# Layer norms of the next batch's x tiles: two at each of two head-group boundaries instead of four inside the first head group

## The chip, the cores and the metric

The kernel runs on one core of a Trainium2 chip. The metric is the time of one execution on the device, in microseconds (us); the median of several runs is compared. Engines are named as in the profile: PE (TensorE matmul), PEld (its weight load), DVE (VectorE), ACT (ScalarE), POOL (GpSimd), SP (SyncE, which issues all the DMAs).

## The reference

Input x is 8 batches of 512 rows by 512, and so is the context. The reference is two layers; the first step, the only one that the change touches, is a cross attention with 16 heads of 32:

```python
x = x + tanh(g_xattn[0]) * mha(layernorm(x), ctx, ctx, W_Q, b_Q, W_K, b_K, W_V, b_V, W_O, b_O)
x = x + tanh(g_ffn[0]) * bitlinear_ffn(layernorm(x), w_gate, w_up, w_down)
x = x + tanh(g_xattn[1]) * softmax(layernorm(x) @ ctx.T) @ ctx
x = x + tanh(g_ffn[1]) * (mxfp4(layernorm(x)) @ mxfp4(w1).T + bias)

def layernorm(x): m, v = mean(x), var(x); return (x - m) / sqrt(v + 1e-5)
def mha(Q, K, V, ...): q, k, v = Q @ W_Q + b_Q, K @ W_K + b_K, V @ W_V + b_V   # 16 heads of 32
    return softmax(q @ k.T / sqrt(32)) @ v                      # per head; the output projection follows
```

## The kernel before

The program has three stages one after another: `attention_phase` (about the first 880 us), `ffn_phase` and `final_phase`. Only the first is changed.

**The work of a batch.** An x tile is 128 rows of x (T = 4 of them, 256 KB each). It is loaded into one of four `stage` buffers (L288). Its layer norm is step "ln1" (DVE: `bn_stats` L514, `bn_aggr` L519; then four short POOL operations of one column, L580, L581, L584, L587) and step "norm" (ACT, L466, which writes the normed tile back into `stage`). PE transposes it (L344), ACT and DVE split the result into a high and a low part (`xt`, L449, L527). The four context tiles use the same four `stage` buffers after the x tiles, without a norm. Projections Q and K (L360) are made for each of four head groups (G = 4, four heads in each), with three passes each for precision; ACT (L458) and DVE (L535) read them out into `part`, which is written to DRAM (`spill`, L300) and read back, rearranged, into `stack` by three DMAs (`fill`, L308). V is projected in the first head group (L374).

**A head group** has 16 slots. In each PE computes one maximum product `mx` (L385; DVE reduces it to the row maximum, L543) for the next heads but a few, and one score product `sc` (L402; ACT takes the exponential into `probs`, L488). The 16 maxima are transposed (L391), copied by ACT (L479) and sent by a small DMA "mrow" (L314) into row 96 of `stack`, where the next group's scores need them. POOL sums `probs` over the four key tiles into `acc`: 12 additions of 128x512 per group (L597), the first when the fifth exponential is there. After the 16 slots come 16 products with V ("pv", L413) and then "den", the products of `acc` with ones (L423), which need the last POOL addition. DVE then takes reciprocals (L549, four of 128 columns), multiplies (L554), ACT adds the bias (L493), SP stores. "den" is in PE's order ahead of everything of the next group.

**The order of the work** is written out by hand. `Clock` holds steps with a time in units (PERIOD = 160 units for a head group, 640 for a batch; a slot is 8 units). Each engine takes the steps that are its own, adds its own lag (`late`), takes the times modulo 640 and issues them in that order, each behind its semaphore waits; a negative time is work for a later batch. So a step with time -636 is at position 4 of the window of the batch before, which is in head group 0; -827 is at position 453, after the last slot of head group 2. Nothing is issued before what is ahead of it on its engine. Batches 0 and 1 and the last two are written out; batches 1 to 5 of the window counter run in a hardware loop with four branches back.

Positions in a batch's window that matter here: the four groups begin at 0, 160, 320, 480; their pv and den at 128 to 156 behind that. DVE's first reciprocal of a group is 2 units into the next one. On SP the order in group 2 and 3 is: fill (392), store (406), spill (411), mrow (442), spill (448), fill (480), spill (516), load 0 (520), fill (520), load 1 (536), load 2 (552), fill (552), spill (553), store (566), load 3 (568), spill (590), fill (592), mrow for group 0 (602), spill (627), and two fills at 32 and 64 of the next window.

The waits that the text speaks of (all unchanged):

```python
wait_count(pe, acc_done, it, shift, G * (T - 1) * J, (g + 1) * (T - 1) * J)          # den
wait_count(act, ln_rstd, it, shift, T, i + 1)                                         # norm
stage_wait(dve, it, shift, i)                                                         # ln1
sync_wait(sp, held, t_full, it, shift, 2 * T, i - STAGE + 1)                          # load
wait_count(act, spilled[side], it, shift, G, g, 16)                                   # read-out of a projection
```

Of the kernel before, what the change touches and what calls it, by code (L numbers as in the profile page):

```python
# [125 lines left out]
def attention_phase(nc, NB, x, ctx_in, w_q, b_q, w_k, b_k, w_v, b_v, spill, attn_t):  # L126
# [11 lines left out]
    with ExitStack() as ctx:  # L138
        def sb(name, shape, dt):
            return ctx.enter_context(nc.sbuf_tensor("a_" + name, shape, dt))  # L140
# [8 lines left out]
        bias = sb("bias", [P, 3, G], F32)  # L149
# [57 lines left out]
        def ahead(n):  # L207

            return round(slot(int(n // 1)) + (n % 1) * U) - 3 * PERIOD

        at = dict(load=-760, load_step=16, ln1=-636, norm=-612, ln_step=24, tload=6, spill=20, act_norm=3, act_turn=4, dve_turn=8,
                  act_qk=6, dve_qk=11, act_v=8, dve_max=5, act_exp=5, mt=-46, mrow=8, act_mt=3, acc=12, pv=7, den=28,
                  recip=34, recip_step=16, norm_out=98, bias=108, store=118, pool_ln=7)
        tx_at, tc_at = (0, 1.5, 3, 4.5), (10.8, 12.3, 13.8, 15.3)
        qk_at = {(0, Q): 6, (0, K): 16.8, (1, Q): 21.4, (1, K): 26, (2, Q): 30.6, (2, K): 35.2, (3, Q): 39.8, (3, K): 44.4}
        fill_at = {(0, Q): 17, (0, K): 25, (1, Q): 32, (1, K): 37, (2, Q): 41, (2, K): 46, (3, Q): 52, (3, K): 56}
        ck = Clock(G * PERIOD, NB)
        for i in range(T):
            ck.add(at["load"] + i * at["load_step"], 9, "load", i)
            ck.add(at["ln1"] + i * at["ln_step"], 8, "ln1", i)  # L220
            ck.add(at["norm"] + i * at["ln_step"], 8, "norm", i)
            ck.add(ahead(tx_at[i]), 1, "t", i)
            ck.add(ahead(tx_at[i]) + at["tload"], 9, "load", T + i)
            ck.add(ahead(tc_at[i]), 1, "t", T + i)
            for c in range(C):
                ck.add(round(7.4 * (i * C + c)), 2, "v", i, c)
# [1252 lines left out]
def build_program(nc, x, ctx_in, g_xattn, g_ffn, w_q, b_q, w_k, b_k, w_v, b_v, w_o, b_o, w_gate, w_up, w_down,  # L1479
                  w1, bias1, delta_w, delta_act, out):  # L1480

    NB, S, D = x.shape
    spill = nc.dram_tensor("spill", [4, 2, 2, P, S], F32, kind="Internal").ap()
    attn_t = nc.dram_tensor("attn_t", [NB, D // P, P, S], F32, kind="Internal").ap()
    x_mid = nc.dram_tensor("x_mid", [NB, S, D], F32, kind="Internal").ap()
    attention_phase(nc, NB, x, ctx_in, w_q, b_q, w_k, b_k, w_v, b_v, spill, attn_t)
    clear_semaphores(nc)
    with ExitStack() as keep1:
        banks = [keep1.enter_context(nc.psum_tensor(f"bank{n}", [P, 512], F32)) for n in range(8)]  # L1490
        with ExitStack() as keep0:
            layer0, layer1 = prepare_weights(nc, banks, keep0, keep1, w_gate.shape[0], w_o, b_o, w_gate, w_up, w_down, w1, bias1,
                                             delta_w, delta_act, g_xattn, g_ffn)
            ffn_phase(nc, NB, banks, {**layer0, **layer1}, x, attn_t, x_mid)
        final_phase(nc, NB, banks, layer1, x_mid, ctx_in, out)
# [27 lines left out]
```

## Time and profile before

| | us |
|---|---|
| median of 3 runs | 1857.91 |
| lowest, highest | 1854.94, 1865.76 |
| the profiled execution, its own time | 1863.25 |
| its span, first to last instruction | 1861.5 |
| busy: PE, DVE, POOL, ACT | 1575.9, 1330.4, 898.3, 868.4 |
| mean granted TensorE clock | 0.929 of full speed |

An engine's busy time is the sum of its instructions; in the attention stage PE is busy some 90% of each batch's 105 us. A row of the timeline gives start, duration, engine, line, operation, tiles and count, and in brackets the idle time of the engine just before it with what ended it. DMA share is the busy share of the 16 DMA engines; at about 1 they are full.

### The profile page before, as it was taken

To read this page: it belongs to the slowest core of one execution; us is meant where nothing else is said; L and a number is where in the kernel's file an instruction comes from. 1 tells how busy PE (TensorE), PEld (TensorE's weight loads), DVE (VectorE), ACT (ScalarE), POOL (GpSimd) and SP (SyncE) were. 2 spreads that over 40 slices of the span, in tenths; PEclk is the share of its full clock that TensorE was granted. 3 is DMA by queue.
4 is the path that set the end of the run, shared out by engine and by line. 5 is a ranking of instruction groups with operands and counts; after the bars stand their busy time and mean duration, and the time that the engine had idled before them with its cause. 6 is when DMAs were issued, how large, how long until landed. Compare 5 with 4: busy or idle time off the path is not lost. (4 is left out here: it accounts for less than half of the span.)

```text
span 1861.5 us, 27434 instructions
## 1 busy us (share of the span) xinstructions
PE 1575.9 (85%) x7400; PEld 1010.4 (54%) x7433; DVE 1330.4 (71%) x2277; ACT 868.4 (47%) x1433; POOL 898.3 (48%) x1098
## 2 busy tenths in 40 slices
PE   5889898989988899997257999999997588878886
PEld 3656555655655556652254544544443476666664
DVE  3676666757676667764755888888885488989886
ACT  3354545545554546544474545555453334444431
POOL 3265665656665666666002323223230366666653
PEclk9899998999999998997588999999998799999998
DMA  5627272543637272620802444444442212111110
GB/s 181 182 81 208 64 205 62 152 130 114 164 102 187 63 206 73 168 71 12 323 24 75 111 108 101 105 106 108 104 99 65 80 52 68 69 63 68 64 51 34
DMA packets 192668, 200.15 MB, mean 108 GB/s; under 512 B 94508, under 2 KB 111416, under 8 KB 192056
## 3 DMA queue, kind: packets, MB, share of 16 engines
q1 hardware_dynamic: 192568, 199.06, 38.4%
q8 instruction: 33, 0.54, 0.1%
q14 instruction: 67, 0.55, 0.1%
HBM read 119.05 MB, written 58.72 MB: 96 GB/s over the span
## 5 line engine op out<-in xcount | busy, mean ns | idle before, releaser
L488 ACT ACTIVATE a_probs<-a_sc 128x512 f32<-128x512 f32 x512 | 301.1, 596 | 330.5 <-PE a_sc L402 282.1
L543 DVE TENSOR_REDUCE a_negmax<-a_mx 128x1 f32<-128x512 f32 x512 | 337.5, 676 | 109.3 <-PE a_mx L385 107.3
L597 POOL TENSOR_TENSOR a_acc<-a_acc,a_probs 128x512 f32<-128x512 f32 x256 | 319.8, 1281 | 6.9 <-ACT a_probs L488 5.5
L597 POOL TENSOR_TENSOR a_acc<-a_probs 128x512 f32<-128x512 f32 x128 | 162.0, 1284 | 222.7 <-ACT a_probs L488 221.8
L385 PE MATMUL a_mx<-a_stack 96*128 96x512 f32 x512 | 230.2, 450 | 31.3 <-DVE a_negmax L543 19.5
L402 PE MATMUL a_sc<-a_stack 97*128 97x512 f32 x512 | 219.9, 432 | 29.5 <-DMA a_stack<-a_mrow 18.7
L962 PE MATMUL bank<-w_wgu,b_xq 128*128 128x512 bf16 x1022 | 230.7, 379 | 11.6 <-ACT b_sig L1001 10.5
L549 DVE RECIPROCAL a_attn<-a_den 128x128 f32<-128x128 f32 x128 | 120.8, 948 | 150.4 <-PE a_den L423 150.4
L962 PEld LDWEIGHTS bank<-w_wgu,b_xq 128*128 128x128 bf16 x1024 | 97.4, 98 | 139.9 <-ACT b_sig L1001 25.7
L385 PEld LDWEIGHTS a_mx<-a_stack 96*128 96x128 f32 x512 | 102.8, 201 | 103.7 <-DVE a_negmax L543 53.7
L1107 POOL TENSOR_TENSOR b_veps<-b_mv,w_eps 128x1 f32<-128x1 f32 x32 | 6.1, 190 | 298.6 <-DVE b_mv L1028 298.6
L402 PEld LDWEIGHTS a_sc<-a_stack 97*128 97x128 f32 x512 | 104.2, 204 | 59.9 <-ACT a_probs L488 22.1
L360 PE MATMUL a_work<-a_xt,a_w_q 128*128 128x512 f32 x384 | 121.6, 431 | 12.2 <-DVE a_xt L527 12.2
L1319 ACT ACTIVATE c_y<-c_xr,c_nbias,c_rstd 128x512 f32<-128x512 f32 x32 | 26.0, 813 | 221.1 <-POOL c_nbias L1456 221.1
L969 PE MATMUL bank<-w_wd,b_hq 128*128 128x512 bf16 x481 | 112.4, 386 | 10.8 <-DMA b_hq<-b_hcode 8.7
L1005 ACT ACTIVATE b_hid<-b_hid,b_htok 128x2048 f32<-128x2048 f32 x32 | 64.1, 2002 | 120.7 <-DVE b_htok L1079 120.7
L413 PE MATMUL a_pvb<-a_probs,a_v 128*32 128x512 f32 x1024 | 120.0, 610 | 0.0
L374 PE MATMUL a_work<-a_w_v,a_ct 128*128 128x512 f32 x384 | 117.8, 421 | 0.0
L951 PE MATMUL bank<-w_wo,b_apart 128*128 128x512 f32 x384 | 105.1, 425 | 12.2 <-POOL b_apart L1102 12.2
L1060 DVE TENSOR_TENSOR b_hid<-b_sig,bank 128x512 f32<-128x512 f32 x128 | 87.3, 683 | 38.5 <-ACT b_sig L1001 38.5
L360 PE MATMUL a_work<-a_ct,a_w_k 128*128 128x512 f32 x384 | 112.2, 403 | 1.5 <-DVE a_ct L527 1.5
L1284 PE MATMUL bank<-c_cn,c_pt 128*128 128x512 f32 x384 | 98.9, 407 | 5.6 <-issue 2.6
(175 smaller groups left out, 2974.7 us busy)
## 6 DMA issues: line engine op xcount, KB each, us to landing
a_stack<-spill SPq DMA_DIRECT2D x192, 256.0 KB, 4.9
spill<-a_part SPq DMA_DIRECT2D x64, 512.0 KB, 3.2
a_stage<-in_x_dram SPq DMA_DIRECT2D x32, 256.0 KB, 5.6
a_stage<-in_ctx_dram SPq DMA_DIRECT2D x32, 256.0 KB, 2.7
attn_t<-a_attn SPq DMA_DIRECT2D x32, 256.0 KB, 2.1
b_xin<-in_x_dram SPq DMA_DIRECT2D x32, 256.0 KB, 2.8
b_araw<-attn_t SPq DMA_DIRECT2D x32, 256.0 KB, 3.1
x_mid<-b_xo SPq DMA_DIRECT2D x32, 256.0 KB, 2.0
```

Source lines behind the costliest of these rows:

```text
L360: last = nc.tensor.matmul(turns.bank("qk", g, side)[:], w["qk"[side]][:, c, a, g * P:(g + 1) * P], src[:, c, m, :], start=c == 0 and n == ...
L374: last = nc.tensor.matmul(turns.bank("v", i)[:], ct[:, c, a, i * P:(i + 1) * P], w["v"][:, c, m, :], start=c == 0 and n == 0, stop=c == C ...
L385: nc.tensor.matmul(mx[i % 2][:], stack[0:96, g, Q, j, t * P:(t + 1) * P], stack[0:96, g, K, j, :], start=True, stop=True).then_inc(mx_full, 1)
L402: nc.tensor.matmul(sc[i % 2][:], stack[0:97, g, K, j, k * P:(k + 1) * P], stack[0:97, g, Q, j, :], start=True, stop=True).then_inc(s_full, 1)
L413: last = nc.tensor.matmul(pvb[DH * j:DH * (j + 1), :], v[:, k, h * DH:(h + 1) * DH], probs[:, k, j, :], start=k == 0, stop=k == T - 1)
L488: nc.scalar.activation(probs[:, k, j, :], sc[i % 2][:], ACT.Exp, scale=SCALE).then_inc(exp_done, 1)
L543: nc.vector.tensor_reduce(negmax[:, g % 2, j, t:t + 1], mx[i % 2][:], axis=AX.X, op=ALU.max, negate=True).then_inc(mx_done, 1)
L549: nc.vector.reciprocal(attn[:, g % 2, q * P:(q + 1) * P], den[:, q * P:(q + 1) * P]).then_inc(recip_done, 1)
L597: nc.gpsimd.tensor_tensor(acc[:, j], probs[:, 0, j] if k == 1 else acc[:, j], probs[:, k, j], ALU.add)\
L951: last = nc.tensor.matmul(bank_o[:], apart[:, t % 2, a, c, :], wo[:, c, m, :], start=c == 0 and n == 0, stop=c == C - 1 and n == 2)
L962: last = nc.tensor.matmul(bank[:], xq[:, t % 2, c, :], wgu[:, side, c, m * 512:(m + 1) * 512], start=c == 0, stop=c == C - 1)
L969: last = nc.tensor.matmul(bank_d[:], hq[:, t % 2, r, :], wd[:, r, :], start=r == 0, stop=r == R - 1)
```

## The change

The loads of the four x tiles are put at -860, -850, -740, -730 instead of -760 to -712 in steps of 16; ln1 at -827, -822, -667, -662 instead of -636 to -564 in steps of 24; norm at -796, -786, -636, -626 instead of -612 to -540. POOL's lag for ln1 is 9 units instead of 7. In positions of a batch's window: loads 420 and 430 (group 2), 540 and 550 (group 3), all of the batch after next; ln1 on DVE 453, 458 (behind group 2's slots) and 613, 618 (behind group 3's); on POOL 462, 467, 622, 627; norm on ACT 487 and 497 (between the first exponentials of group 3), 7 and 17 (the same in group 0). Before, ln1 was at 4, 28, 52, 76 on DVE, 11, 35, 59, 83 on POOL and norm at 31, 55, 79, 103 on ACT, all in group 0.

```diff
-        at = dict(load=-760, load_step=16, ln1=-636, norm=-612, ln_step=24, tload=6, spill=20, act_norm=3, act_turn=4, dve_turn=8,
+        at = dict(load=(-860, -850, -740, -730), ln1=(-827, -822, -667, -662), norm=(-796, -786, -636, -626), tload=6, spill=20, act_norm=3, act_turn=4, dve_turn=8,
                   act_qk=6, dve_qk=11, act_v=8, dve_max=5, act_exp=5, mt=-46, mrow=8, act_mt=3, acc=12, pv=7, den=28,
-                  recip=34, recip_step=16, norm_out=98, bias=108, store=118, pool_ln=7)
+                  recip=34, recip_step=16, norm_out=98, bias=108, store=118, pool_ln=9)
...
         for i in range(T):
-            ck.add(at["load"] + i * at["load_step"], 9, "load", i)
-            ck.add(at["ln1"] + i * at["ln_step"], 8, "ln1", i)
-            ck.add(at["norm"] + i * at["ln_step"], 8, "norm", i)
+            ck.add(at["load"][i], 9, "load", i)
+            ck.add(at["ln1"][i], 8, "ln1", i)
+            ck.add(at["norm"][i], 8, "norm", i)
```

## Rows read from the trace of the kernel before

**Rows 1.** Windows: head group 0 of batches 3, 6 and 7
```profile
core 0: us, PE busy (x) PEld busy (x) DVE busy (x) ACT busy (x) POOL busy (x), PEclk, DMA share, GB/s
380.00:412.00 32.00, 26.41 (x129) 17.20 (x121) 17.56 (x29) 14.50 (x26) 18.78 (x28) 0.95 0.38 90
693.00:723.00 30.00, 26.31 (x133) 17.31 (x125) 17.28 (x29) 14.47 (x26) 19.14 (x28) 0.94 0.40 97
794.70:818.40 23.70, 23.70 (x129) 16.36 (x125) 14.59 (x21) 12.11 (x22) 15.08 (x12) 1.00 0.39 90
```

**Rows 2.** Timeline of PE: pv and den of group 0, batches 3 and 7
```profile
407.08 3.64 PE L413 MATMUL a_pvb<-a_probs,a_v 128*32 128x512 f32 x32
412.50 1.06 PE L423 MATMUL a_den<-a_acc,a_ones 128*32 128x512 f32 x8 [1.78 <-POOL a_acc L597]
...
814.90 3.64 PE L413 MATMUL a_pvb<-a_probs,a_v 128*32 128x512 f32 x32
818.36 1.04 PE L423 MATMUL a_den<-a_acc,a_ones 128*32 128x512 f32 x8
```

**Rows 3.** Groups by line: all den of the attention stage
```profile
L423 PE MATMUL a_den<-a_acc,a_ones 128*32 128x512 f32 x256 | 33.6, 597 | 16.9 <-POOL a_acc L597 16.8
```

**Rows 4.** Timeline of POOL in group 0 of batch 7
```profile
802.59 5.03 POOL L597 TENSOR_TENSOR a_acc<-a_probs 128x512 f32<-128x512 f32 x4 [9.18 <-ACT a_probs L488]
807.59 10.28 POOL L597 TENSOR_TENSOR a_acc<-a_acc,a_probs 128x512 f32<-128x512 f32 x8
```

**Rows 5.** Timeline of PE: group 0's first scores, batches 6, 3 and 0
```profile
697.19 0.50 PE L402 MATMUL a_sc<-a_stack 97*128 97x512 f32 x1 [1.86 <-DMA a_stack<-a_mrow]
...
389.56 0.50 PE L402 MATMUL a_sc<-a_stack 97*128 97x512 f32 x1 [2.79 <-ACT a_probs L488]
...
73.84 0.77 PE L402 MATMUL a_sc<-a_stack 97*128 97x512 f32 x1 [8.15 <-DMA a_stack<-a_mrow]
```

**Rows 6.** Timeline of SP: groups 2 and 3
```profile
451.06 0.38 SPq L300 DMA_DIRECT2D spill<-a_part  x1
...
363.85 0.37 SPq L288 DMA_DIRECT2D a_stage<-in_x_dram  x1
...
378.90 0.52 SPq L314 DMA_DIRECT2D a_stack<-a_mrow  x1
```

**Rows 7.** Windows: around the new places of the loads, and the boundary to group 0
```profile
453.50:455.00 1.50, 0.93 (x4) 0.80 (x5) 0.40 (x1) 0.09 (x1) 1.50 (x2) 1.00 0.96 370
455.00:456.50 1.50, 1.50 (x9) 1.14 (x8) 1.02 (x3) 1.48 (x4) 1.50 (x2) 1.00 0.01 1
...
374.50:376.00 1.50, 1.50 (x8) 1.13 (x8) 1.11 (x2) 0.66 (x3) 1.50 (x2) 1.00 1.06 292
```

**Rows 8.** Timeline of ACT: end of group 3, start of group 0, batches 3 and 6
```profile
377.38 0.69 ACT L458 ACTIVATE a_part<-a_work,a_bias 128x512 fp32r<-128x512 f32 x1 [0.26 <-DMA spill<-a_part]
388.91 1.08 ACT L488 ACTIVATE a_probs<-a_sc 128x512 f32<-128x512 f32 x2 [10.85 <-issue]
...
697.73 0.60 ACT L488 ACTIVATE a_probs<-a_sc 128x512 f32<-128x512 f32 x1 [6.64 <-PE a_sc L402]
```

**Rows 9.** Timeline of DVE: the boundaries, and one ln1
```profile
381.59 0.96 DVE L549 RECIPROCAL a_attn<-a_den 128x128 f32<-128x128 f32 x1 [2.75 <-PE a_den L423]
382.47 0.64 DVE L514 BATCH_NORM_STATS2 a_stats<-a_stage 128x6 f32<-128x512 f32 x1
383.29 0.18 DVE L519 BATCH_NORM_AGGREGATE a_mv<-a_stats 128x2 f32<-128x6 f32 x1 [0.19 <-DVE a_stats L514]
...
462.50 0.96 DVE L549 RECIPROCAL a_attn<-a_den 128x128 f32<-128x128 f32 x1 [4.77 <-PE a_den L423]
```

**Rows 10.** Groups by line: ACT's norm
```profile
L466 ACT ACTIVATE a_stage<-a_stage,a_nbias,a_rstd 128x512 f32<-128x512 f32 x32 | 25.6, 807 | 0.0
```

**Rows 11.** Windows: the clock after the stalls, batch 6 group 0 and batch 3 group 1
```profile
699.00:700.00 1.00, 1.00 (x4) 0.77 (x3) 1.00 (x2) 0.60 (x1) 0.00 (x0) 0.50 1.07 225
...
423.00:424.00 1.00, 1.00 (x4) 0.71 (x4) 0.28 (x2) 0.00 (x0) 0.00 (x0) 0.50 0.00 0
```

## The prediction

> **What bounds the kernel now.** I read the page's slices first (PE is busy nearly throughout the attention stage), then the times at which PE starts "den", group by group, because PE's order puts it ahead of all of the next group. Group 0 takes 6 to 9 us longer from den to den than groups 2 and 3, except in batch 7. Three windows from den to den show it: batch 3, in the loop, 32 us with 26.4 us of PE busy; batch 6, written out, 30 us; batch 7, 23.7 us, all of it PE at full clock [rows 1]. Batch 7 is the control that the trace holds: no batch comes after it, so its group 0 has no layer norm in it, and group 3 ahead of it no x load. What is lost in the others falls into four pieces.
> (a) den waits for POOL. In batch 3 den starts 5.42 us after pv, in batch 7 3.46 us after it: 1.96 us lost [rows 2]. Over the stage PE's idle time ahead of den is 16.9 us, nearly all put down to POOL [rows 3]; seven of its waits, of 1.78 to 2.11 us, are group 0 of batches 0 to 6.
> (b) The first score of group 0 waits for the mrow DMA: 1.86 us in batch 6, 8.15 us in batch 0 [rows 5]; 1.5 to 2.4 us in batches 1 to 4, none in batch 7. The DMA engines are full there (share 1.06, [rows 7]) and stay so from about 364 to 390 us, so what lands is set by the bytes ahead of it.
> (c) In the batches entered by a branch back (2 to 5), ACT does nothing for 10.85 us after its last instruction of the body, and PE waits for it, 2.79 us in batch 3; batch 6, entered without a branch back, has ACT idle only for want of a score [rows 5, 8].
> (d) After each stall the clock falls to half (1.2 of 2.4 GHz) for some 3 us; the granted clock was 0.50 at 699 and at 423 us [rows 11].
>
> **The change part by part.** All sums are made against the profiled execution (1863.25 us, span 1861.5), which is 5.3 us above the median of 1857.91; I apply the difference to the median.
>
> *ln1 on POOL, out of group 0.* POOL is busy 19.14 us in group 0 of batch 6 against 15.08 us in batch 7, for four norms: 1.0 us each [rows 1]. Two of the four stand between the 12 additions, whose chain is then the last to end. Without them the chain is that of batch 7: it runs 802.59 to 817.87, 15.3 us, and den starts at 818.36, so POOL is through 0.5 us before PE wants it [rows 2, 4]. In the loop batches a slower start of PE's slots leaves POOL more room, not less. So (a) goes wholly: 7 x about 2.0 = 14 us. What is late next is PE itself. The same POOL work now stands behind the last addition of groups 2 and 3, where POOL has nothing for 6 to 9 us (9.18 us before its first addition of batch 7 [rows 4]): 2.1 us in it costs nothing. The lag of 9 instead of 7 changes no neighbour there.
>
> *ln1 on DVE.* One costs 0.64 + 0.19 + 0.18 = 1.0 us [rows 9]. Two at a boundary are 2.0 us; DVE is idle before the first reciprocal for 4.77 us behind group 2 and for 2.75 us behind group 3, plus about 1.2 us before the last read-out of a projection, into which the third norm fits [rows 9]. Cost 0. Were that cover gone, the reciprocal and the first maximum behind it would be late by what is over, and PE's maximum product two slots on after that.
>
> *norm on ACT.* 0.81 us each [rows 10], now between the first exponentials of a group. Two exponentials, two norms and a third exponential are 3.2 us (0.54 each), three PE slots 3.5 us: PE is not held. A slot is 1.18 us (batch 7: 23.7 us less 3.5 of pv and 1.2 of den, by 16). The read-out of projection (2, Q) behind them starts about 0.3 us later. I take 0, between 0 and 0.3 x 7 = 2 us.
>
> *The loads of tiles 0 and 1, from group 3 to group 2.* On SP they now stand behind the store and the spill that is issued at 451.06 and ahead of mrow 3 [rows 6]. Their own wait (context tiles transposed) was met in group 1. The DMA engines are busy until 455 and then idle for about 3 us (share 0.01, [rows 7]); 512 KB at the 200 to 370 GB/s seen take 1.4 to 2.6 us, so they land by about 458. DVE asks for tile 0 at about 457.7 and must be through by 462.5: room for a load some 2.5 us later. What is queued behind DVE's wait is the reciprocal and the maxima of group 3, and PE behind these. Nothing that SP puts after them (mrow 3, needed at 462.6) loses its slack.
>
> *Group 3's transfers.* Loads 0, 1, 3 were issued there from 363.85 on, between fills and spills, all ahead of mrow at 378.90 [rows 6]. Now two of four are: 512 KB less ahead of mrow, 1.4 to 2.6 us; 256 KB less ahead of the spill that ACT's last read-out and one fill wait for, about 1 us. So mrow lands about 2 us sooner and (b) goes in batches 1 and 6 (1.6 and 1.9 us) and shrinks by about 2 us in batch 0: 5.5 us; bounds 0 (if mrow's place in the order of issue holds it, not the bytes ahead) and 6. In batches 2 to 5 PE then waits for ACT all the same; there only ACT's earlier arrival counts, 0.26 us (batch 3's wait, [rows 8]) to 1.2 us: 1.5 us over four, bounds 0 and 3.
>
> *The clock.* In batch 6 group 0 was about 5.7 us longer than in batch 7 (den to den, to a tenth; the windows are rounded to 30 and 23.7): 5.7 = 2.0 (den) + 1.9 (mrow) + 1.8, which only the half clock leaves. With no stall I expect no fall in batches 1 and 6: 3.5 us. The fall in group 1 (batch 3 at 423) comes behind den's wait and two waits for DVE of 1.3 and 1.7 us that stay; group 1 is bound by DVE as much as by PE, so I count nothing of it, at most 1.5 x 7 = 10 us.
>
> *Sum:* 14 + 5.5 + 1.5 + 3.5 - 1 (read-outs, start-up) = 23.5 us, which I take down to 22, as the smaller terms rest on each other. 1857.9 - 22 = 1836 us. Own range 1829 to 1846.
>
> **The branch back.** The row is ACT's 10.85 us, in four of seven boundaries and only where there is a branch [rows 8]; DVE, whose last instruction of the body ends at 378.84, has its next at 381.59, so its branch costs at most 2.75 us, hidden by the wait for den [rows 9]. The Trainium skill, "Runtime: NRT & Kernel Launch", section "Instruction fetch mechanics", says that a taken branch whose target is not among the two pages of instructions held forces a fetch of the page before the engine can go on. ACT's row agrees; by that rule the change, which moves instructions in every engine's body and in what precedes the loop, could make DVE one of those that fetch.
>
> **The rivals.**
> *The wait alone goes.* The mrow and clock terms stay as they are, because mrow is issued behind a fill that waits for its own spill; then 14 us less small costs: 1844 us. For it: (b) has two causes in a row. Against it: batch 7, which lacks the x loads in the group ahead and has neither.
> *More goes.* ACT's stall shortens with the queue 2 us shorter (4 x 2 = 8 us) and the clock stays up in group 1 (up to 10 us): about 1823. For it: the transfers end at 390 us, just after ACT comes back at 388.91. Against it: ACT's idle time is 10.4 to 10.9 us from its arrival, whatever the time of arrival.
> *Nothing.* What group 0 gives, group 1 takes: its DVE-bound start (recips, the maxima and the x splits) or new waits in group 3 for ACT: 1857. Against it: everything of group 1 is ordered behind den, so it moves up with it.
> *Slower: DVE's branch becomes a fetch.* DVE reaches its branch some 1 us later than now, at about 379.9 (ln1 of tile 3 is the last of its body). If it then stands still as ACT does, 10.9 us, its first maximum of group 0 ends at about 392.4 and PE's third product of the group, at 386.4 now, resumes there: about 3.5 us more than today's wait for ACT in each of four batches, 14 us, and the kernel would still gain. If the fetches of both engines go one after the other, DVE is back at about 400 and PE 12 us later than now: 48 us. The change loses from about 5.5 us a batch on, that is when DVE stands for over 13 us. Middle of the two, 31 us: 1858 - 22 + 31 = 1867.
>
> **How the numbers follow.** Forecast 1836: 0.50. The wait alone, 1844: 0.20. More, 1823: 0.12. Nothing, 1857: 0.10. Slower, 1867: 0.08. What a measurement of this kernel can tell is about 0.5%, 9.3 us. Faster by over that (below 1848.6): 0.50 + 0.12 + 0.17 of the 0.20 = 0.79; within it: 0.03 + 0.10 = 0.13; slower: 0.08. The range 1825 to 1856 leaves out half of "more", part of "nothing" and "slower".
>
> **What would show it.** PE's den of group 0 starts 3.46 us behind pv in all batches, with no idle time from POOL; its first score in batches 1 and 6 without a wait for mrow and the clock at 1.0 from 693 on; group 0 at about 24 us in batches 1 and 6, about 29.5 us in batches 2 to 5, with ACT's 10 to 11 us there still; DVE's ln1 of tiles 0 and 1 without a wait for the load, its reciprocals still behind den. Wrong, if POOL still ends after pv, if a reciprocal starts over 1 us behind den, if ACT's norm waits with exponentials behind it, or if "issue" idle time appears on DVE.

## The result and the profile after

| | before | after |
|---|---|---|
| median, us | 1863.0 (6 runs) | 1816.84 (6 runs) |
| lowest, highest | 1854.94, 1865.76 | 1813.73, 1818.08 |
| ratio after / before | | 0.9758 (95%: 0.9735 to 0.9781) |
| span of the profiled execution | 1861.5 | 1816.3 |

The kernel is 46 us faster by the medians (45.2 us by the two profiled spans); the forecast was 22 us (1836), and the measured time lies under its range of 1825 to 1856. All of it is in the attention stage: its last den starts at 834.30 us instead of 879.91. The windows of group 0 of batches 3, 6 and 7, from den to den, answer to [rows 1]:

```profile
core 0: us, PE busy (x) PEld busy (x) DVE busy (x) ACT busy (x) POOL busy (x), PEclk, DMA share, GB/s
364.90:388.30 23.40, 23.40 (x127) 16.30 (x122) 14.59 (x21) 13.33 (x24) 15.93 (x15) 1.00 0.40 104
653.60:676.90 23.30, 23.30 (x125) 16.26 (x121) 14.59 (x21) 13.28 (x24) 15.86 (x15) 1.00 0.44 107
748.90:772.50 23.60, 23.60 (x129) 16.32 (x125) 14.59 (x21) 12.12 (x22) 15.09 (x12) 1.00 0.38 90
```

The reader is to see that batches 3 and 6 are now as batch 7 was all along: PE is busy for the whole window, at full clock. Batch 6 (written out) lost 6 us, as forecast; batch 3 (in the loop) lost 8.6 us, where 2.5 were forecast. PE's timeline in batch 3, pv and den, for [rows 2]; and all den and all first scores by line, for [rows 3] and the waits of [rows 5]:

```profile
384.83 3.64 PE L413 MATMUL a_pvb<-a_probs,a_v 128*32 128x512 f32 x32
388.29 1.04 PE L423 MATMUL a_den<-a_acc,a_ones 128*32 128x512 f32 x8
...
L402 PE MATMUL a_sc<-a_stack 97*128 97x512 f32 x512 | 216.1, 424 | 9.3 <-DMA a_stack<-a_mrow 7.3 <-ACT a_probs L488 1.7
L423 PE MATMUL a_den<-a_acc,a_ones 128*32 128x512 f32 x256 | 33.4, 593 | 2.4 <-POOL a_acc L597 2.4
```

Den follows pv by 3.46 us, and its idle time fell from 16.9 to 2.4 us. The score's wait for mrow is 7.3 us in all, 6.98 of it in batch 0. ACT's timeline at the branch back into batch 3's group 0, for [rows 8]:

```profile
361.58 0.69 ACT L458 ACTIVATE a_part<-a_work,a_bias 128x512 fp32r<-128x512 f32 x1
367.52 0.60 ACT L488 ACTIVATE a_probs<-a_sc 128x512 f32<-128x512 f32 x1 [5.25 <-PE a_sc L402]
368.01 0.80 ACT L466 ACTIVATE a_stage<-a_stage,a_nbias,a_rstd 128x512 f32<-128x512 f32 x1
```

```profile
q14 instruction: 67, 0.55, 0.1%
```
```profile
q14 instruction: 47, 0.39, 0.1%
```

Twenty packets of 8 KB fewer are five for each of the four branches back. They can be seen at the stall itself: from 377 to 390 us, around ACT's idle time at the boundary to batch 3, the kernel before has three packets of this queue; the changed kernel has none from 361 to 374 us.

```profile
q14 instruction: 3, 0.02, 0.7%
```

### The profile page after: what moved, and what is told of

Its sections match the earlier page's. It is cut to its first block and busy times, and to the rows that moved or that the text cites. A ratio compares the mean times of both kernels' runs of the same rounds, so it can differ in the third digit from the quotient of the medians.

```text
span 1816.3 us, 27472 instructions
## 1 busy us (share of the span) xinstructions
PE 1566.0 (86%) x7433; PEld 1007.0 (55%) x7433; DVE 1332.3 (73%) x2277; ACT 869.0 (48%) x1433; POOL 899.6 (50%) x1098
## 5 line engine op out<-in xcount | busy, mean ns | idle before, releaser
L488 ACT ACTIVATE a_probs<-a_sc 128x512 f32<-128x512 f32 x512 | 301.0, 597 | 302.9 <-PE a_sc L402 291.4
L597 POOL TENSOR_TENSOR a_acc<-a_acc,a_probs 128x512 f32<-128x512 f32 x256 | 320.8, 1284 | 8.2 <-ACT a_probs L488 6.6
L597 POOL TENSOR_TENSOR a_acc<-a_probs 128x512 f32<-128x512 f32 x128 | 161.7, 1286 | 243.4 <-ACT a_probs L488 242.6
L402 PE MATMUL a_sc<-a_stack 97*128 97x512 f32 x512 | 216.1, 424 | 9.3 <-DMA a_stack<-a_mrow 7.3
L969 PE MATMUL bank<-w_wd,b_hq 128*128 128x512 bf16 x512 | 118.8, 386 | 8.7 <-DMA b_hq<-b_hcode 8.7
L374 PE MATMUL a_work<-a_w_v,a_ct 128*128 128x512 f32 x384 | 111.8, 403 | 0.0
```

The costliest lines, as they stand in the source:

```text
L374: last = nc.tensor.matmul(turns.bank("v", i)[:], ct[:, c, a, i * P:(i + 1) * P], w["v"][:, c, m, :], start=c == 0 and n == 0, stop=c == C ...
L402: nc.tensor.matmul(sc[i % 2][:], stack[0:97, g, K, j, k * P:(k + 1) * P], stack[0:97, g, Q, j, :], start=True, stop=True).then_inc(s_full, 1)
L488: nc.scalar.activation(probs[:, k, j, :], sc[i % 2][:], ACT.Exp, scale=SCALE).then_inc(exp_done, 1)
L597: nc.gpsimd.tensor_tensor(acc[:, j], probs[:, 0, j] if k == 1 else acc[:, j], probs[:, k, j], ALU.add)\
L969: last = nc.tensor.matmul(bank_d[:], hq[:, t % 2, r, :], wd[:, r, :], start=r == 0, stop=r == R - 1)
```

## Experiments

Two theories stood after the result. **A, position**: ACT fetches instructions anew at the branch or not, by where the loop's body lies in its instruction list; the change put instructions of batch 2's norms ahead of the loop and so moved the body from 191 to 448 (258 instructions) to 195 to 453 (259; all positions are counted in the compiled list, from 0 and without labels). **B, transfers**: the stall went because group 3 has two x loads fewer. The table gives group 0's length in us, den to den, from one trace of each kernel; the text the medians. e1 to e4 ran beside the kernel before at 1859.8 us, e5 to e8 beside it at 1862.6, so a difference between the two sets is good to some 3 us.

```
                      b1    b2    b3    b4    b5    b6    b7   ACT "issue" idle
before               29.4  32.0  32.0  31.2  33.2  29.3  23.6  10.4 to 10.9 x4
e1 before + 1        27.6  28.4  27.1  27.3  28.0  26.7  23.6  none
e2 before, loads     26.8  31.7  32.1  32.5  32.7  26.0  23.4  10.8 to 11.1 x4
e6 loads + 1         27.1  26.4  26.3  26.3  26.3  25.9  23.6  none
e7 norms first + 1   26.6  25.8  25.6  26.5  25.6  25.4  23.6  none
after                24.1  24.0  23.4  23.4  23.4  23.4  23.6  none
e3 after + 252       23.5  29.4  30.6  29.7  30.1  23.4  23.4  back
e4 after + 124       23.8  30.3  30.5  30.3  30.4  23.6  23.6  back
e5 after + 125       23.8  23.8  23.5  23.4  23.4  23.6  23.6  none
e8 loads earlier     23.6  23.4  23.4  23.4  23.4  23.4  23.6  none
```

**e1 to e5: idle instructions on ACT.** In ACT's `window`, ahead of the wait of step "score" (so that they run while it waits for batch 0's first score); N is 1, 252, 124, 125, the first on the kernel before, the others on the one after. The three lines shift the numbers behind them: L491, L600 in these kernels are L488, L597.

```diff
                         g, i = args
                         k, j = i // J, i % J
+                        if isinstance(it, int) and it + shift == 0 and g == 0 and i == 0:
+                            for _ in range(N):
+                                act.sem_inc(held, 1)
```

> The kernel before, with one idle instruction (a semaphore increment that nobody waits for) more on ACT ahead of the loop; nothing else. Theory A (position): ACT's stall at the branch back hangs on where the loop's body lies in ACT's instruction list. Before, the body was instructions 191 to 448 of the list, after the change 195 to 453; one instruction more moves it to 192 to 449. The stall goes: no idle time of 10 to 11 us put down to issue in batches 2 to 5, group 0 there 29.5 us as in batches 1 and 6 instead of 31.2 to 33.2, in all 4 x 2.6 = 10 us less; POOL's wait ahead of den and the wait for mrow stay. Theory B (transfers): the stall went because the DMA queue is shorter with two x loads gone from group 3; this kernel's transfers are those of before, so the stall stays and the time is that of before within 3 us. The Trainium skill (Runtime: NRT & Kernel Launch, Instruction fetch mechanics) has instructions held in two pages of 256 and a fetch at a branch to a page that is not among them, which is theory A; a body that touches three pages would then fetch, and the same body moved by one may touch two.

Measured: 1842.68 us, ratio to before 0.9906 (0.9879 to 0.9933). One idle instruction takes 17 us off the kernel before. ACT at the boundary to batch 3:

```profile
378.21 0.60 ACT L491 ACTIVATE a_probs<-a_sc 128x512 f32<-128x512 f32 x1 [6.37 <-PE a_sc L402]
```

The stall is gone with every transfer where it was: theory B falls for the stall. The gain is larger than expected (10), since group 0 is 27 to 28.4 us and not 29.5. Windows from den to den show why, here batches 2 and 3 in this kernel:

```profile
273.80:302.20 28.40, 24.27 (x126) 16.01 (x118) 17.23 (x29) 14.51 (x26) 19.25 (x28) 1.00 0.40 104
374.50:401.60 27.10, 24.29 (x126) 16.02 (x118) 17.23 (x29) 14.51 (x26) 19.24 (x28) 1.00 0.41 100
```

The clock stays at 1.00, where it was 0.90 to 0.95 in group 0 of batches 1 to 6, and PE's busy time in group 0, summed over batches 1 to 7, is 168.9 us instead of 179.6. So about half of what group 0 gave is the clock. Batches 1 and 6, which have no branch ahead of them, gained it too, although mrow's wait is still there; in batch 2 it is even 2.16 us, and no fall follows:

```profile
278.11 0.49 PE L402 MATMUL a_sc<-a_stack 97*128 97x512 f32 x1 [2.16 <-DMA a_stack<-a_mrow]
```

Why the clock stayed up in those two batches isn't shown.

> The changed kernel with 252 idle instructions more on ACT, while it waits for batch 0's first score. ACT's loop body is then instructions 447 to 705 of its list instead of 195 to 453. Theory A, with pages of 256 and a list that begins 64 into a page (the only offset at which the body of before touches three pages and that of after two): the body touches three pages again, the stall of 10 to 11 us is back in four batches, and the time rises by 4 x 3 to 6 us = 12 to 25 us, beside up to 8 us for the idle instructions themselves in batch 0. Theory B: only those up to 8 us, no stall.

Measured: 1846.77 us, ratio 0.9934 (0.9909 to 0.9958), 30 us above the changed kernel; the stall is back in batches 2 to 5 with the layer norms and loads of the changed kernel. Batch 0's den is 9 us later than after (107.67 us), by the idle instructions.

> The changed kernel with 124 idle instructions more on ACT in the same place; the control of the one with 252. Theory A with pages of 256: the body (319 to 577) touches two pages, no stall, the time is that of the changed kernel plus up to 3 us. Theory A with blocks of 128 instructions and a body that must lie in three: it touches four, the stall is back, 12 to 25 us more. Theory B: no stall.

Measured: 1836.5 us, ratio 0.9872 (0.9848 to 0.9896): the stall is back here too, so the pages of 256 that I had taken for theory A don't fit, and either the blocks are of 128 or the idle instructions do harm by themselves (rival C). The next run was to tell:

> The changed kernel with 125 idle instructions on ACT where 124 brought the stall back; one more. Theory A with blocks of 128 (the instruction queue's packets are of 8 KB, 128 instructions of 64 bytes; the list begins 64 into a block): a body that touches four blocks is fetched anew at each branch (before 255 to 512, plus 124 383 to 641, plus 252 511 to 769), one that touches three is not (after 259 to 517, before plus one 256 to 513). Plus 125 is 384 to 642, three blocks: no idle time of ACT put down to issue in batches 2 to 5, group 0 there 23.4 us, time 1817 to 1821 us, some 18 us below the kernel with 124. Rival C (the idle instructions themselves make the loop slow to start, whatever the position): the time stays at 1836 us and the stall with it.

Measured: 1816.91 us, ratio 0.9754 (0.9725 to 0.9782), the time of the changed kernel. ACT at the boundary to batch 3 in the kernel with 124, then with 125:

```profile
380.48 0.60 ACT L491 ACTIVATE a_probs<-a_sc 128x512 f32<-128x512 f32 x1 [10.96 <-issue]
```
```profile
368.65 0.60 ACT L491 ACTIVATE a_probs<-a_sc 128x512 f32<-128x512 f32 x1 [5.34 <-PE a_sc L402]
```

One instruction, in the unrolled part ahead of the loop, is worth 20 us, and rival C falls. The six positions (three with the stall, three without) agree with one rule: blocks of 128 instructions, the list beginning 64 into a block, a stall when the body touches four of them, none at three. The queue's packets follow it in all ten kernels: 67 to 69 where the stall is (before, e2, e4, e3), 47 to 49 where it isn't. The block is the size of these packets (0.39 MB in 47). The offset of 64 is inferred from the six positions, not seen. Nor are they enough to exclude other rules: all three stalls have the body begin in the last place of a block, and blocks of 64 from the list's beginning, with a stall at six of them and none at five, fit as well. For 128 speaks the packets' size.

One more loop bears on it, which the change doesn't touch. DVE's loop of the final stage has 309 instructions (1330 to 1638 of its list, four blocks by the rule) and one branch back. DVE stands there in each of the ten traces; in the kernel before:

```profile
1652.45 0.69 DVE L1368 BATCH_NORM_STATS2 c_stats<-c_xr 128x6 f32<-128x512 f32 x1 [2.15 <-issue]
```

It is 2 us (1.87 to 2.70 in the ten) and not 11. The windows of ACT's stall and of this one differ in the DMA share, 1.07 and 0.02:

```profile
378.00:388.90 10.90, 7.26 (x50) 3.31 (x42) 6.01 (x10) 0.06 (x1) 2.21 (x6) 1.00 1.07 275
1650.30:1652.45 2.15, 2.15 (x11) 1.75 (x10) 0.00 (x1) 0.00 (x0) 0.00 (x0) 1.00 0.02 5
```

So whether an engine stands hangs on the position; how long may well hang on how full the DMA engines are. These are two engines and two loops, and no run varied the transfers enough to tell: in e2 the share is 1.06 through the stall too.

**e2 and e6: the loads alone.** The kernel before with the change's load times; e6 has e1's one instruction as well.

```diff
-        at = dict(load=-760, load_step=16, ln1=-636,
+        at = dict(load=(-860, -850, -740, -730), ln1=-636,
...
-            ck.add(at["load"] + i * at["load_step"], 9, "load", i)
+            ck.add(at["load"][i], 9, "load", i)
```

> The kernel before with the change's load times alone (-860, -850, -740, -730); ln1 and norm stay in group 0, and ACT's instruction list is the one of before. Theory A: the stall of 10 to 11 us at the branch back stays in batches 2 to 5; mrow's wait goes in batches 1 and 6 (1.6 and 1.9 us) with the clock's fall behind it, some 7 us less in all. Theory B: the stall shrinks or goes, 15 to 25 us less. POOL's wait ahead of den stays by both.

Measured: 1856.32 us, ratio 0.9981 (0.9969 to 0.9994), 3.5 us, where both theories wanted more. By the table batches 1 and 6 gain 2.6 and 3.3 us and the loop batches nothing, as there PE waits for ACT anyhow; the stall is whole, so theory B falls here too:

```profile
383.48 1.08 ACT L488 ACTIVATE a_probs<-a_sc 128x512 f32<-128x512 f32 x2 [11.12 <-issue]
```

> The kernel before with the change's load times and one idle instruction on ACT: what the change is without its layer norms' new places. With the stall gone the loads count in every batch: mrow's wait goes in batches 1 to 6, so 4 to 10 us less than the kernel with the one instruction alone (1842.7), at 1833 to 1839 us; POOL's wait ahead of den stays whole (16.9 us). If the transfers matter only where the profile puts a wait down to mrow, 4 us; if the clock's fall behind the wait goes too, 10 us. What is left to the changed kernel's 1816.8 is the layer norms' part, predicted at 14 us.

Measured: 1831.72 us, ratio 0.9836 (0.9804 to 0.9869), 11 us below e1 (13 by the ratios). The same edit is worth 3.5 us with ACT's stall and 11 to 13 without. The waits for mrow, by line, in e1 (15.8 us) and in e6 (8.2, nearly all of it batch 0's):

```profile
L402 PE MATMUL a_sc<-a_stack 97*128 97x512 f32 x512 | 217.3, 427 | 17.8 <-DMA a_stack<-a_mrow 15.8 <-ACT a_probs L491 1.9
```
```profile
L402 PE MATMUL a_sc<-a_stack 97*128 97x512 f32 x512 | 218.1, 428 | 10.1 <-DMA a_stack<-a_mrow 8.2 <-ACT a_probs L491 1.7
L423 PE MATMUL a_den<-a_acc,a_ones 128*32 128x512 f32 x256 | 33.9, 602 | 18.5 <-POOL a_acc L600 18.5
```

From e6 to the changed kernel it is 15 us, the layer norms' places.

**e7: POOL's part of the norms ahead of its additions**, on the kernel before with one idle instruction.

```diff
-        at = dict(load=-760, load_step=16, ln1=-636, norm=-612, ln_step=24,
+        at = dict(load=-760, load_step=16, ln1=-636, norm=-612, ln_step=8,
```

> The kernel before with one idle instruction on ACT and the four layer norms in steps of 8 units instead of 24, still in group 0: POOL's positions are 11, 19, 27, 35, all ahead of its first addition at 44; the loads are those of before. Theory of the prediction (POOL's chain of 12 additions with two norms in it ends late): POOL's wait ahead of den goes, 1.96 us in each of 7 batches, 14 us below the kernel with the one instruction alone (1842.7), 1829 us. Rival (DVE's and ACT's load of group 0 is what counts, not POOL's order): the same work sits there still, and closer together; no gain, or 2 to 4 us more.

Measured: 1832.75 us, ratio 0.9835 (0.9801 to 0.987), 10 us below e1 (13 by the ratios) where 14 were expected. POOL in batch 3, from the last norm on, and PE's pv and den:

```profile
379.66 0.19 POOL L590 TENSOR_TENSOR a_nbias<-a_nmean,a_rstd 128x1 f32<-128x1 f32 x1
379.81 5.14 POOL L600 TENSOR_TENSOR a_acc<-a_probs 128x512 f32<-128x512 f32 x4
384.91 10.16 POOL L600 TENSOR_TENSOR a_acc<-a_acc,a_probs 128x512 f32<-128x512 f32 x8
...
391.93 3.64 PE L413 MATMUL a_pvb<-a_probs,a_v 128*32 128x512 f32 x32
395.38 1.04 PE L423 MATMUL a_den<-a_acc,a_ones 128*32 128x512 f32 x8
```

With no norm between the additions POOL is through at 395.07 and den follows pv by 3.45 us: in this batch den's wait was POOL's order. Group 1 gives some back: it takes 25.6 to 26.2 us in most batches, 24.9 to 26.2 in e1.

**e8: a version beyond the change.** Two lines of times on the changed kernel:

```diff
-        at = dict(load=(-860, -850, -740, -730), ln1=(-827, -822, -667, -662), norm=(-796, -786, -636, -626), tload=6,
+        at = dict(load=(-960, -940, -860, -850), ln1=(-827, -822, -667, -662), norm=(-776, -766, -636, -626), tload=6,
```

> The changed kernel with all four x loads ahead of group 3 (-960, -940, -860, -850, positions 320, 340, 420, 430), and the norms of tiles 0 and 1 at -776 and -766, behind the read-out of projection (2, Q) instead of ahead of it. No x load is left in the full stretch of the DMA engines. In the steady batches nothing waits for mrow any more, so 0 there; in batch 0 mrow's wait (6.98 us) shrinks by 1 to 2 us and ACT's read-out is no longer held 1.5 us by the first norm: 1 to 3 us less than 1816.8 in all. Rival: the norms between later exponentials or the loads beside group 2's first fills cost as much; 1815 to 1819.

Measured: 1807.86 us (1807.78 to 1808.32), ratio 0.9709 (0.9682 to 0.9737), 9 us below e5, which ran beside it and has the changed kernel's time. It is faster than the expectation and its rival had it. Batch 0's den starts at 95.03 instead of 98.45 us; PE's first score, in the changed kernel and here:

```profile
74.11 0.77 PE L402 MATMUL a_sc<-a_stack 97*128 97x512 f32 x1 [6.98 <-DMA a_stack<-a_mrow]
```
```profile
70.76 0.77 PE L402 MATMUL a_sc<-a_stack 97*128 97x512 f32 x1 [5.45 <-DMA a_stack<-a_mrow]
```

By den's starts in one trace each, this kernel against the changed one, 6.8 us are in the attention stage, 3.4 of them in batch 0. The rest is spread over batches, and some 3 us lie behind that stage, which the edit doesn't touch; what part of them is chance was not tested. Nor are the two edits told apart.

## Why the prediction was right or wrong

*What failed: the branch back.* The step reads "in batches 2 to 5 PE then waits for ACT all the same", worth 1.5 us over the four in the sum, and its list of signs "with ACT's 10 to 11 us there still". I had the row, and I had the rule beside it, but used the rule for DVE alone, as a danger, and took ACT's stall as fixed. What the runs show in its place: the stall went with ACT's position alone, and in e1, where nothing else was changed, group 0 of batches 2 to 5 is 17.6 us shorter by the table (128.4 to 110.8), part of it PE's wait for ACT and part the clock. Two facts that pointed to it were to be had before: the body is longer than 256 instructions, and the change moves norms of a further batch ahead of the loop. They say that the stall could change; that it would go was not to be read from them. In the chain of kernels before, e1, e6, after (1863, 1842.7, 1831.7, 1816.8) the stall's going is 17 to 20 us, the loads 11 to 13, the norms 15. The forecast for the last two, clock with them, was 23.5 before rounding; measured 26 to 28. That this is close is in part luck, since the clock of batches 1 and 6, 3.5 us of the forecast, came back already in e1.

*The rule.* The Trainium skill, "Runtime: NRT & Kernel Launch", section "Instruction fetch mechanics", has a taken branch outside the held pages force a fetch. The runs agree (e1, e4, e5). It gives pages of 256 instructions, two of them held; by that e4's body (319 to 577 of its list, 383 to 641 with the offset of 64, two pages) would not stall, and it does; no other offset puts the body before in three pages and that after in two. For ACT the measurement decides against pages of 256, and blocks of 128 fit.

*The slower rival* (DVE's branch becomes a fetch) did not happen. DVE in the changed kernel at the boundary to batch 3, for [rows 9]:

```profile
362.97 0.68 DVE L514 BATCH_NORM_STATS2 a_stats<-a_stage 128x6 f32<-128x512 f32 x1
363.84 0.18 DVE L519 BATCH_NORM_AGGREGATE a_mv<-a_stats 128x2 f32<-128x6 f32 x1 [0.19 <-POOL a_nmean L580]
366.04 0.96 DVE L549 RECIPROCAL a_attn<-a_den 128x128 f32<-128x128 f32 x1 [2.02 <-PE a_den L423]
```

The reciprocal starts 1.1 us behind den, as before; the two norms sit in idle time.

*"More goes"* came nearest in size (1823) with the wrong cause: it shortened the stall by a shorter DMA queue, and e2 shows the stall at its full 10.8 to 11.1 us with that queue, e1 none of it with the long one. Its other half, the clock up in group 1, didn't come either.

*POOL's wait: right.* 14 us forecast; den's idle time fell by 14.5 us [rows 3]. POOL in the changed kernel, additions of group 3 of batch 2, the norm behind them, additions of the next group 0, for [rows 4]:

```profile
353.53 10.01 POOL L597 TENSOR_TENSOR a_acc<-a_acc,a_probs 128x512 f32<-128x512 f32 x8
363.49 0.20 POOL L580 TENSOR_TENSOR a_nmean<-a_mv,a_minus 128x1 f32<-128x1 f32 x1
...
372.84 5.04 POOL L597 TENSOR_TENSOR a_acc<-a_probs 128x512 f32<-128x512 f32 x4 [6.90 <-ACT a_probs L488]
377.83 10.16 POOL L597 TENSOR_TENSOR a_acc<-a_acc,a_probs 128x512 f32<-128x512 f32 x8
```

*Mrow in group 0: right in batches 1 and 6*, and worth more than put down, because with the stall gone it counts in the loop too (e2 against e6). *The clock in group 0* stayed up as forecast, but the link is not as written: item (d) has it fall after each stall, and in e1 it doesn't fall after mrow's waits of 0.7 to 2.2 us in batches 1 to 6. Loads on SP in group 2 and group 3, and mrow, for [rows 6]; the full queue at the boundary, for [rows 7]:

```profile
331.60 1.42 SPq L288 DMA_DIRECT2D a_stage<-in_x_dram  x2
...
350.26 1.06 SPq L288 DMA_DIRECT2D a_stage<-in_x_dram  x2
...
362.24 0.52 SPq L314 DMA_DIRECT2D a_stack<-a_mrow  x1
```
```profile
358.00:359.50 1.50, 1.50 (x8) 0.88 (x7) 1.50 (x4) 0.60 (x1) 1.50 (x2) 1.00 1.05 302
```

Mrow is issued 2.7 us ahead of den of group 3 (364.93) instead of 1.6 us; the DMA engines are still full, only less far behind.

*Batch 0: wrong.* Four us were forecast, two for den and two for mrow; 0.56 came. Den's two came: it follows pv by 3.45 us instead of 5.53. Mrow's wait fell by 1.2 us (8.15 to 6.98), but PE reached it later. The norms of the next batch now stand in ACT's order ahead of projection read-outs of the start-up:

```profile
51.24 0.81 ACT L466 ACTIVATE a_stage<-a_stage,a_nbias,a_rstd 128x512 f32<-128x512 f32 x1 [4.50 <-POOL a_nbias L587]
```

The read-out behind them is at 53.15 instead of 51.59 us, and PE's first score at 74.11 instead of 73.84. The rest, 1.25 us, is lost between the first score and pv, where the clock is at half for longer: from 74 to 78 us it is 0.50 instead of 0.62, from 78 to 82 us 0.74 instead of 1.00. Why is open.

*Group 1's clock: right to count nothing.* It still falls there, behind the same two waits for DVE (1.27 and 1.65 us), for [rows 11]:

```profile
399.00:400.00 1.00, 1.00 (x4) 0.81 (x3) 0.41 (x1) 0.00 (x0) 0.00 (x0) 0.50 0.00 0
```

## What to carry to other kernels

Before forecasting an edit in a kernel with hardware loops, count each engine's instructions up to and in the loop: idle time put down to "issue", only behind branches, is not a constant of the kernel, and an edit anywhere ahead of the loop can make or remove it. Try one idle instruction ahead of the loop on such an engine, and some more if one changes nothing: here one was enough because the body of 258 began, by the rule, just at an edge, and a longer body may need a larger shift. 125 of them, where the engine waits anyhow, cost nothing in the time (1816.91 against 1816.84 us). An edit's worth is read with the longest wait of its stretch in place: the loads gave 3.5 us behind ACT's stall and 11 to 13 without it.
